# Long attention: score products dealt over three groups of rows, query scores in head order 2, 0, 3, 1

## What is computed

```python
scores = jnp.einsum('bhqd,bhkd->bhqk', Q, K) / jnp.sqrt(jnp.float32(D_K))
attn = jax.nn.softmax(scores, axis=-1)
out = jnp.einsum('bhqk,bhkd->bhqd', attn, V)
out = out.transpose(0, 2, 1, 3).reshape(B, S, D)
out = jnp.einsum('bsd,ed->bse', out, w_o) + b_o
return _layer_norm(x + out, ln_g, ln_b)
```

## Time and profile before

| | us |
|---|---|
| median of three runs | 4217.46 |
| the profiled execution | 4211.42 |
| its span, first to last instruction | 4209.6 |
| TensorE busy in the span | 3890.5 |
| VectorE busy | 3375.9 |
| ScalarE busy | 2736.0 |
| GpSimd busy | 2091.0 |
| slots 0 to 255, first exponential 3626.1, last 4093.4 | 468 |

### The profile page before, as it was taken

One profiled execution on the slowest core, in us unless ns is written; L12 is line 12 of the kernel. 1 busy time (PEld: TensorE's weight loads), 2 busy tenths in 40 slices (PEclk: granted clock), 3 DMA queues, 4 the chain that ended last, 5 costly groups with the idle time before them and its releaser, 6 DMA issues.

```text
span 4209.6 us, 151591 instructions
## 1 busy us (share of the span) xinstructions
PE 3890.5 (92%) x65521; PEld 2422.8 (58%) x65521; DVE 3375.9 (80%) x6704; ACT 2736.0 (65%) x4940; POOL 2091.0 (50%) x1202
## 2 busy tenths in 40 slices
PE   6999999999999999589999999999999987899985
PEld 3666666666666666456666666666666654333333
DVE  7988888888888888588888888888888875577745
ACT  4767767777677676157777676776777752366662
POOL 4656656566666565066566565665656630000000
PEclk9999999999999999799999999999999997599997
DMA  4112121121121211111121211212111110000000
GB/s 101 40 34 55 40 55 37 38 58 36 40 55 40 55 35 39 27 28 40 34 59 41 55 35 40 55 40 54 37 38 37 36 32 1 0 1 1 1 1 10
DMA packets 131142, 153.71 MB, mean 37 GB/s; under 512 B 67480, under 2 KB 90408, under 8 KB 128816
## 3 DMA queue, kind: packets, MB, share of 16 engines
q1 hardware_dynamic: 130480, 144.02, 15.0%
HBM read 35.93 MB, written 1.05 MB: 9 GB/s over the span
## 4 chain that ended last, share of the span: by engine, by line
PE 63%; DVE 24%; issue 7%; ACT 4%; POOL 0%; DVEq 0%; SPq 0%; POOLq 0%; DMA 0%; ACTq 0%
PE psum L377 10%; DVE turn L658 9%; PE psum L446 8%; PE psum L388 8%; PE psum L413 6%; DVE den L716 5%; PE psum L438 4%; DVE nmax L694 4%; PE psum L366 4%; PE psum L1274 3%; PE psum L509 3%; PE psum L1262 3%; PE psum L516 3%; PE psum L526 3%; PE psum L1264 2%
## 5 line engine op out<-in xcount | busy, mean ns | idle before, releaser
L658 DVE TENSOR_TENSOR turn<-psum,ropes 128x512 f32<-128x512 f32 x1536 | 938.5, 673 | 6.2 <-POOL qkr L783 4.2
L790 POOL TENSOR_TENSOR turn<-turn 128x1024 f32<-128x1024 f32 x384 | 903.2, 2373 | 25.7 <-DVE turn L658 25.7
L545 ACT ACTIVATE sq<-psum 128x512 f32<-128x512 f32 x768 | 456.1, 594 | 541.8 <-PE psum L366 541.8
L802 POOL TENSOR_TENSOR scratch<-scratch,rden 128x1024 f32<-128x1024 f32 x192 | 365.3, 1903 | 883.0 <-DVE rden L719 883.0
L366 PE MATMUL psum<-wqkv,xT 128*128 128x512 f32 x1536 | 767.7, 623 | 31.8 <-DVE turn L658 30.2
L783 POOL TENSOR_TENSOR qkr<-turn,rn 128x1024 f32<-128x1024 f32 x384 | 728.1, 1917 | 19.6 <-DVE rn L679 19.4
L388 PEld LDWEIGHTS psum<-ident,qkr 128*128 128x128 f32 x3072 | 335.1, 143 | 347.1 <-issue 166.0
L377 PE MATMUL psum<-wqkv,xT 128*64 128x512 f32 x1536 | 433.8, 644 | 65.3 <-DVE turn L658 53.5
L388 PE MATMUL psum<-ident,qkr 128*128 128x128 f32 x3072 | 473.6, 288 | 7.6 <-POOL qkr L783 6.8
L684 DVE TENSOR_REDUCE ss<-sq 128x16 f32<-128x1024 f32 x384 | 448.9, 1211 | 0.0
L425 PEld LDWEIGHTS psum<-scratch,Vs 64*64 64x64 f32 (+1 forms) x12288 | 327.0, 134 | 183.0 <-issue 180.6
(11 more groups left out here) (191 smaller groups left out, 6420.1 us busy)
## 6 DMA issues: line engine op xcount, KB each, us to landing
Vs<-V SPq DMA_DIRECT2D x384, 128.0 KB
Vs<-V SPq DMA_DIRECT2D x768, 64.0 KB
wqkv<-in_L_ffn_Wqkv_dram SPq DMA_DIRECT2D x12, 1536.0 KB
wo<-in_L_ffn_Wo_dram SPq DMA_DIRECT2D x48, 128.0 KB
zs<-Y SPq DMA_DIRECT2D x192, 31.8 KB
w<-in_L_ffn_W_dram SPq DMA_DIRECT2D x12, 341.0 KB
zs<-Y SPq DMA_DIRECT2D x168, 0.2 KB
w<-in_L_ffn_W_dram SPq DMA_DIRECT2D x12, 128.0 KB
```

Source lines behind the costliest of these rows:

```text
L545: act.activation(sq[:, q // 2, q % 2, :, :], bank[QK_BANK[q]][:, :].rearrange("p (h d) -> p h d", d=RH), ACT.Square).then_inc(sem("squared ...
L658: e = dve.tensor_tensor(dst, src, tab.unsqueeze(1).broadcast_to([P, HEADS, RH]), ALU.mult)
L790: pool.tensor_tensor(t1, t1, turn2[:, w, :, :, :].rearrange("p a h d -> p (a h d)"), ALU.add).then_inc(sem("added"), 1)
```

## The change

`scores2` is cut in two calls, one for each h, and `scores_by_key` is cut into the key product and `less_max`. In a slot TensorE's order becomes: projection if any, turned maxima or turned sums if any, query h0, key of both tiles, query h1, less of the first tile, the weighing, less of the second. Unit u takes head 2, 0, 3, 1 in place of 0, 1, 2, 3, and VectorE writes its maxima to the column of that head. The number of instructions and their shapes stay as they are.

```diff
+        UNIT_ROWS = (2, 0, 3, 1)
...
-            def scores2(u):
-                n, t, r = u // 32, u // 4 % 8, u % 4
-                if u % 32 == 0:
-                    pe.wait_ge(sem("at_stacked"), 2 * n + 2)
-                if u >= 2:
-                    pe.wait_ge(sem("at_maxed"), u - 1)
-                for h in range(2):
...
+            def scores2(u, h):
+                n, t, r = u // 32, u // 4 % 8, UNIT_ROWS[u % 4]
+                if h == 0:
+                    if u % 32 == 0:
+                        pe.wait_ge(sem("at_stacked"), 2 * n + 2)
+                    if u >= 2:
+                        pe.wait_ge(sem("at_maxed"), u - 1)
...
+            def less_max(v):
+                i, r = v // 32, v % 4
+                b = RING_OF["st", v]
                 pe.matmul(bank[b][:, :], onesr[32 * r:32 * r + 32, :], mrow[i % 2][32 * r:32 * r + 32, :],
                           start=False, stop=True).then_inc(sem("at_st"), 1)
...
-                if max_unit(j) is not None:
-                    scores2(max_unit(j))
+                u, tiles = max_unit(j), exp_tiles(j)
                 if max_section(j) is not None:
                     turn_max(max_section(j))
                 if out_section(j) is not None:
                     turn_out(out_section(j))
-                tiles = exp_tiles(j)
-                for v in tiles[0:1]:
+                if u is not None:
+                    scores2(u, 0)
+                for v in tiles:
                     scores_by_key(v)
+                if u is not None:
+                    scores2(u, 1)
+                if tiles:
+                    less_max(tiles[0])
                 if weighed(j) is not None:
                     weigh(weighed(j))
-                for v in tiles[1:2]:
-                    scores_by_key(v)
+                if tiles:
+                    less_max(tiles[1])
...
-                    i, c, b = u // 16, P * (u // 4 % 4) + 32 * (u % 4), S2_BANK[u % 2]
+                    i, c, b = u // 16, P * (u // 4 % 4) + 32 * UNIT_ROWS[u % 4], S2_BANK[u % 2]
```

More of the change, by code:

```diff
@@ L1234, in project @@
                     sem("at_proj"), 1)
-            def scores2(u):
-                n, t, r = u // 32, u // 4 % 8, u % 4
-                if u % 32 == 0:
-                    pe.wait_ge(sem("at_stacked"), 2 * n + 2)
-                if u >= 2:
-                    pe.wait_ge(sem("at_maxed"), u - 1)
-                for h in range(2):
-                    mm = pe.matmul(bank[S2_BANK[u % 2] + h][:, :], qst[n % 2][32 * r:32 * r + 32, P * t:P * t + P],
-                                   kst[n % 2][32 * r:32 * r + 32, 512 * h:512 * h + 512], start=True, stop=True)
-                mm.then_inc(sem("at_scores"), 1)
+            def scores2(u, h):
[5 more added lines that the diff above has]
+                        pe.wait_ge(sem("at_maxed"), u - 1)
+                mm = pe.matmul(bank[S2_BANK[u % 2] + h][:, :], qst[n % 2][32 * r:32 * r + 32, P * t:P * t + P],
+                               kst[n % 2][32 * r:32 * r + 32, 512 * h:512 * h + 512], start=True, stop=True)
+                if h:
+                    mm.then_inc(sem("at_scores"), 1)
             def turn_max(i):
```

## The result

The changed kernel takes 4282.77 us, the median of six runs (4263.58 to 4293.93), where the kernel before takes 4217.49 (six runs, 4200.23 to 4219.9). The ratio is 1.0157, with a 95% interval from 1.0137 to 1.0177. The prediction of 4219, range 4200 to 4242, was wrong.

What follows compares the result with a forecast made beforehand. It took a loop through ScalarE and three banks, not TensorE's products, as the bound. Terms +2.1, +7.4, +11.0, -8.6, -1.4, -8.8 sum to +1.7 us; against the median 4217.5 that gives 4219, range 4200 to 4242.

Steps and rivals of the forecast that it cites:

- the part on the clock: First eleven slot pairs: low clock could return sooner under denser products; bounds none to -16 us; a later fall meant error.
- The undisturbed pair: High-clock slot pairs without extra work: 3.08 us instead of 3.05, +.03 each over 70 pairs, +2.1 us.
- The copy of sums: 14 pairs with ScalarE's copy between exponentials: key d waits for a's exponential, +.53 each, +7.4 us.
- Turned sums: 13 pairs: the maximum and all behind it start later, 7 by 1.01 and 6 by .66, +11.0 us.
- Projections: Six projection groups: second projection starts earlier, -1.25 us, and the pair before gives -.2; together -8.6 us.
- The low clock pair: Pairs at the low clock: 4.55 us instead of 4.88; -2.6 over 8, some +1.2 for three others, -1.4 us.
- The clock's first return: Opening slots: high clock comes back six pairs sooner, before slot 20, each saving 1.47 us, -8.8 us.
- Rival 1: Opening slots: clock returns where it did before, so no gain from it; +10.5, 4228 us; chance .24.
- Rival 2: Pairs: dealing out shared array rows frees .6 us each over 60, 36 us less, 4183; chance .11 with another fast case.
- Rival 3: Odd slots: weight loads queue after the second key wait, .1 to .2 us a pair, about 4243; chance .15.
- Rival 4: Head order and tiles were already on different rows in three of four slots; only waits count; .50 shared with 4219.

## Why the prediction was wrong, point by point

**The step that failed** is in the part on the clock. It reckoned only with the level at the stage's beginning and how soon it would come back, and took for granted that it would stay high afterwards: a fall stood in the text as a sign of error and in no rival, with no chance and no price. The trace of before had a hint that this wants an argument. Its pairs at the low clock had records covering 47.60 of 48 us and still didn't bring the level up, so records in place were no warrant that the level would hold. The two places that I made longer, 13 pairs by .66 to 1.01 us and 14 by .53, were costed as chains alone. What the runs showed in its place: the level fell nine times in the slots, and half a microsecond and one put into the wait for `at_o` in the kernel before, 7 and 15 us in all, cost 68 and 104.

**The undisturbed pair** (+.03): right, 3.08. **The copy of sums** (+.53): the pair ahead of the second one shown is 3.57 long (3807.44 to 3811.01), right; but in the run with the query products first its price at slot 242 was 11 us by the clock of the last slots, where the forecast has .5 for it. **Turned sums** (1.01 and .66): right to .05 at the high clock, by 5.18. **Projections** (-8.6 for six groups): right; a section with them takes 31.47 at the high clock, one without 27.71, where it was 31.40 and 26.49. From such sections, and the two before the last (27.72 for 26.15), the chains of slots 32 to 239 add up to about 11 us at the high clock, against the 11.9 summed (2.1 + 7.4 + 11.0 - 8.6). **The low clock pair** (4.55): mis-sized. By the starts of the weighings, pairs take 4.52 and 4.92 in turn, 4.72 on average, so half of the -.33 came:

```profile
3638.70 1.90 PE L1280 MATMUL psum<-turn,scratch 128*9 128x512 f32 x8
...
3643.62 1.90 PE L1280 MATMUL psum<-sq,scratch 128*9 128x512 f32 x8
...
3648.14 1.04 PE L1280 MATMUL psum<-turn,scratch 128*9 128x512 f32 x4
```

**The clock's first return** (six pairs earlier): it came at slot 12 in place of 21, in the changed kernel and in four others with its order in the first slots. But it is no fixed thing: it came at slot 3 with the head order alone, at slot 5 with the key order alone, and at slot 14 in the run with the 1 us memset, whose first 20 slots are those of the kernel before. Slots 0 to 31 are 7.6 us shorter, so the term of -8.8 was borne out in sign; that the denser products earned it isn't shown. What followed, 87.6 us the other way in slots 32 to 255, was in the sum with its chains alone. An estimate from the rows: some 184 us more at the low level, each losing (4.72 - 3.08) / 4.72, is 64 us; with the 11 of the chains it makes 75 of the 80.

**The rivals.** Rival 1 kept the clock as it was and is off by 55 us. Rival 2 had a gain from parting shared rows; the head order alone gives none in the median, and .37 us in a projection pair. The rule of the Trainium skill beside it ("TensorE: Matmul & The Clock Gate", Part 3: products start and end strictly in program order) is against the trace here too: of the list query h1, key, key, in the undisturbed pair of the kernel before, the keys start at 3710.03 and query h1 at 3710.36. Rival 3, slower by weight loads that queue, had the right sign by luck and a wrong mechanism: key d, query h1 and less c pass their gate together (3796.31) and the weighing follows .43 later, so the loads run side by side. Rival 4 was right in that parting the rows brings next to nothing. None of the four had a fall of the clock.

## What to carry to other kernels

A wait put on TensorE is not priced by its own length when the clock can fall in it: ask of each lengthened wait what TensorE has done in the microseconds around it, and give the fall a chance and a price (here 4.72 - 3.08 = 1.64 us for each pair until the level is back). Look for it in pairs that a change stretches by half a microsecond too. Full records are no warrant in a stage of products on 32 of the 128 rows; whether the rows are the reason wasn't tested. Where a wait can't be shortened, a useless product in it can be worth more than it costs, and what lets the waiting product go, two short operations on another engine, is worth putting ahead of a long one.

## What the hardware showed beyond what I had expected

The clock fell with a TensorE pause of 1.57 us, and with one of .81 in the run with the .5 us memset. The Trainium skill ("TensorE: Matmul & The Clock Gate", HAM oscillation) tells of such falls between dense bursts of products, with longer pauses. Here the products around the pause use a quarter of the rows each, and the short ones were enough.

Whether it falls changes from section to section with the same list: nine of fourteen turned sums in one execution. And it doesn't go by the pause alone. With .81 us it fell in five of six sections with a stacking step (the .5 us memset), with .95 in none of the same six (query products first); and with 1.18 in every section it fell in all of these six, but in one of the seven others (turned sums moved alone). In the first two the pair takes 5.04 and 4.80 us; what decides isn't shown.

Once low, it can last through pairs whose records leave almost no gap: 27 us in after, and 58 in the run with the .5 us memset, all of them covered:

```profile
3781.80:3839.80 58.00, 58.00 (x228) 21.95 (x220) 26.72 (x25) 25.48 (x47) 0.00 (x0) 0.50 0.00 1
```

The mean clock of the slots went from 0.94 to 0.80 by 7 us of memsets on VectorE. The projections' slots, with products on all 128 rows, are a tenth of the slots, and three of after's eight returns behind a fall came in them. What exactly the chip weighs isn't told by these runs; work in the wait and a shorter wait both kept the level at the turned sums.
